# A gated cross-attention and feed-forward block: order of GpSimd's sums and statistics, of one copy on ScalarE and of two normalizations on VectorE

## What is computed

```python
x = x + jnp.tanh(g_xattn[0]) * xattn(layernorm(x), ctx, Wq, bq, Wk, bk)
x = x + jnp.tanh(g_ffn[0]) * ffn(layernorm(x), W_up, W_gate, W_down)

def xattn(logits, features, Wq, bq, Wk, bk):
    query = einsum('bnc,dc->bnd', features, Wq) + bq
    key = einsum('bnc,dc->bnd', features, Wk) + bk
    attention = softmax(einsum('bnd,bmd->bnm', query, key), axis=-1)
    return einsum('bln,bmn->blm', logits, attention)

def ffn(x, W_up, W_gate, W_down):   # each weight w rounded to sign * mean(|w|), or 0
    up, gate = einsum('bsd,ed->bse', x, wu), einsum('bsd,ed->bse', x, wg)
    return einsum('bse,de->bsd', silu(up) * gate, wd)
```

## Time and profile before

| | us |
|---|---|
| median of three runs | 396.83 (396.21 to 397.08) |
| profiled execution, its own time | 397.08 |
| its span | 395.3 |
| TensorE busy | 389.9 (99%) |
| VectorE busy | 314.4 (80%) |
| ScalarE busy | 266.7 (67%) |
| GpSimd busy | 169.3 (43%) |

### The profile page before, as it was taken

How to read it: one execution, slowest core, us unless ns; L and a number is a source line. 1 busy time by engine, 2 the same in 40 slices (tenths; PEclk the granted TensorE clock), 3 DMA queues, 4 the chain that set the end, 5 groups by cost and what they waited for, 6 DMA issues and landing times.

```text
span 395.3 us, 6059 instructions
## 1 busy us (share of the span) xinstructions
PE 389.9 (99%) x1944; PEld 214.9 (54%) x1952; DVE 314.4 (80%) x475; ACT 266.7 (67%) x360; POOL 169.3 (43%) x187
## 2 busy tenths in 40 slices
PE   8999999999999999999999999999999999999997
PEld 6566775454444444444444444444445565656886
DVE  0768897888899985879897875786869989798974
ACT  3786989889778786869788863746377566654400
POOL 0686826657875013222347002435359446271000
PEclk9999999999999999999999999999999999999999
DMA  7999967598500030030009643041500000000014
GB/s 286 409 413 414 389 210 174 151 266 211 162 2 0 1 108 0 2 107 0 2 0 225 117 79 61 1 167 73 165 22 1 2 2 2 0 2 0 2 55 159
DMA packets 43183, 43.91 MB, mean 111 GB/s; under 512 B 30992, under 2 KB 33168, under 8 KB 41104
## 3 DMA queue, kind: packets, MB, share of 16 engines
q1 hardware_dynamic: 43152, 43.53, 35.4%
HBM read 29.89 MB, written 6.29 MB: 92 GB/s over the span
## 4 chain that ended last, share of the span: by engine, by line
PE 75%; DVE 7%; issue 6%; ACT 5%; POOL 3%; DMA 2%; SPq 1%; DVEq 0%; POOLq 0%; ACTq 0%
PE pair L872 22%; PE pair L874 22%; PE pair L946 14%; PE pair L990 11%; PE pair L788 3%; DMA xf<-in_wdT 2%; PE pair L738 1%; ACT sh L1102 1%; DVE small L1473 1%; PE pair L724 1%; PE pair L803 1%; DMA xf<-in_first 1%; SPq L466 1%; DVE small L1515 1%; DVE xf L1674 1%
## 5 line engine op out<-in xcount | busy, mean ns | idle before, releaser
L872 PE MATMUL pair<-xb_hi,w_sb 128*128 128x512 f16 x448 | 169.8, 379 | 0.4 <-ACT xf L1299 0.2
L874 PE MATMUL pair<-xb_lo,w_sb 128*128 128x512 f16 x448 | 169.8, 379 | 0.0
L872 PEld LDWEIGHTS pair<-xb_hi,w_sb 128*128 128x128 bf16 x448 | 43.8, 98 | 52.9 <-ACT xf L1299 1.1
L874 PEld LDWEIGHTS pair<-xb_lo,w_sb 128*128 128x128 bf16 x448 | 43.8, 98 | 51.1 <-issue 0.3
L1250 ACT ACTIVATE xf<-xf,small 128x512 f32<-128x512 f32 x48 | 34.5, 720 | 52.3 <-DVE xf L1669 31.6
L946 PE MATMUL pair<-x_sb,sh 128*128 128x512 bf16 x248 | 55.1, 379 | 0.4
L1674 DVE SCALAR_TENSOR_TENSOR xf<-xf,small 128x512 f32<-128x512 f32 x48 | 40.0, 836 | 8.4 <-ACT xf L1250 8.4
L946 PEld LDWEIGHTS pair<-x_sb,sh 128*128 128x128 f16 x256 | 24.9, 98 | 30.6 <-DVE x_sb L1711 0.9
L604 POOL TENSOR_TENSOR w_sb<-w_sb 128x512 bf16<-128x512 bf16 x8 | 9.6, 1197 | 63.0 <-ACT w_sb L1124 63.0
L1679 DVE TENSOR_TENSOR sh<-xf,sh 128x512 f16<-128x512 f32 x36 | 32.1, 898 | 0.7 <-ACT sh L1261 0.7
L1725 DVE SCALAR_TENSOR_TENSOR x_sb<-pair,small,x_sb 128x256 f32<-128x256 f32 (+1 forms) x57 | 25.5, 472 | 5.9 <-PE pair L990 5.4
(11 more groups left out here) (198 smaller groups left out, 715.9 us busy)
## 6 DMA issues: line engine op xcount, KB each, us to landing
w_sb<-in_wugT SPq DMA_DIRECT2D x8, 1024.0 KB, 14.7
x_sb<-in_x SPq DMA_DIRECT2D x4, 1024.0 KB, 11.3
xf<-in_wdT SPq DMA_DIRECT2D x4, 1024.0 KB, 6.6
xt_sb<-in_wdT SPq DMA_DIRECT2D x4, 1024.0 KB, 5.0
xt_sb<-in_xT SPq DMA_DIRECT2D x12, 256.0 KB, 6.1
x_dram<-x_sb SPq DMA_DIRECT2D x8, 256.0 KB, 3.3
out<-x_sb SPq DMA_DIRECT2D x8, 256.0 KB, 2.0
x_sb<-x_dram SPq DMA_DIRECT2D x2, 1024.0 KB, 5.5
```

Source lines behind the costliest of these rows:

```text
L872: pe.matmul(dst[:, m * 512:(m + 1) * 512], w[:, o:o + P], hi[:, k], start=start and k == 0, stop=False, skip_group_check=not start)
L874: last = pe.matmul(dst[:, m * 512:(m + 1) * 512], w[:, o:o + P], lo[:, k], start=False, stop=k == 1, skip_group_check=not start)
```

## The change

It touches no computation, only the order of steps on three engines. On GpSimd the four sums of x are made in one go, in the order in which the products need them (XA follows), and the wait for `s_pn0` between them goes. In batch 1 the second pair of both layer norms, `rstd1_two(1, 1)` and `rstd2_two(0, 1)`, comes before the sums of p. The T1 difference goes from behind T3 to the second round of the loop of batch 2. On ScalarE the copy of T1 goes ahead of `exp_row(3, 2)`. On VectorE `norm_x1(0, 2)` and `norm_x1(0, 3)` go ahead of two reciprocals of batch 2.

```diff
--- before.py
+++ after.py
@@ -251,7 +251,7 @@
         MIX = (1, 5, 6, 3, 7, 2, 4)
         MIX_TO = {1: (0, 0), 5: (1, 1), 6: (0, 1), 3: (0, 1), 7: (1, 1), 2: (0, 0), 4: (1, 0)}
         MIX_BEFORE = {2: 1, 3: 6, 7: 5}
-        XA = {1: (0, 0), 2: (0, 1), 4: (1, 1), 5: 0, 7: 1, 6: 2, 3: 3}
+        XA = {1: (0, 0), 2: (0, 1), 4: (1, 1), 5: 0, 6: 1, 3: 2, 7: 3}
         PB = {1: (0, 0), 2: (1, 0), 3: (1, 1), 5: 0, 6: 1, 7: 2, 4: 3}
 
         def x_quarter(b, lh, nh):
@@ -568,17 +568,15 @@
                 step(pool.tensor_scalar(ve2[:, two], mv2[:, own, 1], LN_EPS, 1.0 / XS ** 2, ALU.add, ALU.mult))
                 pool.tensor_tensor(r2[:, own], ve2[:, two], mhalf, ALU.pow).then_inc(s_r2, 2)
 
-            def x_sums_1(b):
+            def x_sums(b):
                 for i in range(NT):
                     pool.wait_ge(*xt_in(b, i))
                 pool.tensor_tensor(x_sum(b, 0), x_quarter(b, 1, 0), x_quarter(b, 1, 1), ALU.add).then_inc(s_ss, 1)
-                pool.tensor_tensor(x_sum(b, 1), x_quarter(b, 0, 0), x_quarter(b, 1, 0), ALU.subtract).then_inc(s_ss, 1)
-
-            def x_sums_2(b):
                 hold(pool, s_ss, 4 * b + 1)
-                pool.tensor_tensor(x_sum(b, 2), x_sum(b, 0), x_quarter(b, 0, 0), ALU.subtract).then_inc(s_ss, 1)
-                hold(pool, s_ss, 4 * b + 3)
-                pool.tensor_tensor(x_sum(b, 3), x_quarter(b, 0, 1), x_sum(b, 2), ALU.subtract).then_inc(s_ss, 1)
+                pool.tensor_tensor(x_sum(b, 1), x_sum(b, 0), x_quarter(b, 0, 0), ALU.subtract).then_inc(s_ss, 1)
+                hold(pool, s_ss, 4 * b + 2)
+                pool.tensor_tensor(x_sum(b, 2), x_quarter(b, 0, 1), x_sum(b, 1), ALU.subtract).then_inc(s_ss, 1)
+                pool.tensor_tensor(x_sum(b, 3), x_quarter(b, 0, 0), x_quarter(b, 1, 0), ALU.subtract).then_inc(s_ss, 1)
 
             def p_sums_1(b):
                 hold(pool, s_at, b * NT + NT)
@@ -616,31 +614,29 @@
 
             pool.wait_ge(s_tanh, 1)
             pool.wait_ge(s_const, 4)
-            x_sums_1(0)
-            hold(pool, s_pn0, NT - 1)
-            x_sums_2(0)
+            x_sums(0)
             rstd1_two(0, 0)
             p_sums_1(0)
             rstd1_two(0, 1)
             p_sums_2(0)
-            x_sums_1(1)
-            x_sums_2(1)
+            x_sums(1)
             rstd1_two(1, 0)
             rstd2_two(0, 0)
+            rstd1_two(1, 1)
+            rstd2_two(0, 1)
             p_sums_1(1)
-            rstd1_two(1, 1)
             p_sums_2(1)
-            rstd2_two(0, 1)
             rstd1(2, 0)
             rstd1(2, 1)
             rstd2_two(1, 0)
             rstd2_two(1, 1)
             hold(pool, s_x2n, 2 * NT)
             pool.tensor_tensor(t3_sb, xf_half(1, 1), xf_half(1, 0), ALU.subtract).then_inc(s_t3, 1)
-            hold(pool, s_t3, 1)
-            pool.tensor_tensor(xf_half(1, 0), xf_half(1, 0), xf_half(0, 0), ALU.subtract).then_inc(s_t1, 1)
             for b in range(NS, NB - 1):
                 for i in range(NT):
+                    if i == 1:
+                        hold(pool, s_t3, 1)
+                        pool.tensor_tensor(xf_half(1, 0), xf_half(1, 0), xf_half(0, 0), ALU.subtract).then_inc(s_t1, 1)
                     rstd2(b, i)
                     if i + 2 < NT:
                         rstd1(b, i + 2)
@@ -1195,15 +1191,15 @@
                         if b == 1 and i == 2:
                             act.wait_ge(s_x2n, NT)
                             high_t(0, "B11", xf_half(0, 0))
+                        if b == 2 and i == 1:
+                            act.wait_ge(s_t1, 1)
+                            high_t(0, "T1", xf_half(1, 0))
                         exp_row(b + 1, i + 1)
                         if b == 2 and i == 2:
                             copy_at(b + 1, NT - 2)
                             norm_p(b + 1, NT - 1)
                         if i == 1:
                             norm_p(b + 1, 2)
-                        if b == 2 and i == 1:
-                            act.wait_ge(s_t1, 1)
-                            high_t(0, "T1", xf_half(1, 0))
 
                     if first and i in (0, NT - 1):
                         sum_abs(0, 2 + (i > 0))
@@ -1574,14 +1570,14 @@
                 add_mixed(b, 1)
                 row_max(b + 1, 0)
                 row_max(b + 1, 1)
+                if b == 1:
+                    norm_x1(0, 2)
+                    norm_x1(0, 3)
                 row_rsum(b + 1, 0)
                 row_rsum(b + 1, 1)
                 add_mixed(b, 5)
                 rows_in(b + 1, 0)
                 add_mixed(b, 6)
-                if b == 1:
-                    norm_x1(0, 2)
-                    norm_x1(0, 3)
                 row_max(b + 1, 2)
                 rows_in(b + 1, 1)
                 add_mixed(b, 3)
```

## The result

The changed kernel took a median of 400.35 us (399.96 to 401.18, four runs) beside 396.65 for the kernel before (four runs): a ratio of 1.0095, 95% interval 1.0083 to 1.0107. That is 3.70 us slower, by the interval 3.3 to 4.2. The profiled execution took 400.03 for a span of 398.2, with a granted clock of 1.0. The lines have new numbers: the product of the probabilities is L1555 (L1559 before), the first sum of p L583 (L585), T1 L639 (L641), the transposes L745 (L749), the products L784 (L788), exponential and scaling L1098 and L1103, the rounding to 16 bits L1139, the reciprocal L1473, the statistics L1486.

A forecast was written before the change was run, and what follows sets the result against it. The prediction took TensorE, busy 389.9 of 395.3 us, to set the end. Profiled 397.08 - 0.10 + 1.69 + 2.45 = 401.12, or 400.9 against the median of 396.83; range 399.0 to 401.8.

The forecast's parts named there:

- place 1: GpSimd's sums of x in batch 0 made in one go: 0.1 us gained, as they hold up VectorE's products.
- place 2: Second rstd pairs ahead of batch 1's sums of p on GpSimd: TensorE waits 1.60 us, plus 0.09 for restart.
- place 3: norm_x1(0, 2) and (0, 3) ahead of VectorE's reciprocals: costs nothing, covered by the hole of place 2; without it about 0.4.
- place 4: Later T1 on GpSimd, its copy ahead of ScalarE's exponential: TensorE 2.45 us late at the transposes near 79 us.
- The reading as shared bandwidth: Rival at place 1: no exclusive lock between VectorE and GpSimd, most of 0.95 us gained; total 400.0, no chance given.
- only place 4 costs: Rival: batch 1's fourth row tile statistic finished before 38.1, so place 2 costs nothing; 399.2 us, chance 0.04.
- nothing taken back: After 80 us the order is the old one and engines enter equally late, so none of the delay is recovered.
- The slip of SP's queue: Rival: late T3 and T1 meet SP's queue, delaying feed-forward entry by 1 to 2 us more; 402.4, chance 0.07.

The follow-up runs named there:

- experiment 5: The changed kernel with norm_x1(0, 2) and norm_x1(0, 3) back at their old place on VectorE: 400.20 us, ratio 1.0090 to the kernel before.
- experiment 6: The kernel before with the sums of x in one go and new order, batch 0's fourth held behind VectorE's third product: 396.40 us, ratio 0.9992.
- experiment 8: experiment 6 plus T1 behind rstd1(2, 2) on GpSimd, the coefficients one round later, ScalarE's order as before: 396.71 us, ratio 0.9997 to the kernel before.
- experiment 9: experiment 6 with VectorE's remainder of B21 moved behind two normalizations of batch 1: 396.32 us, ratio 1.0000 to the kernel before.
- experiment 7: The changed kernel with only rstd1_two(1, 1) back behind the first sums of p: 398.60 us, ratio 1.0049 to the kernel before.
- experiment 2: The kernel before with only both second rstd pairs put ahead of the sums of p in batch 1: 398.03 us, ratio 1.0027.
- experiment 4: The kernel before with only T1 moved behind the coefficients on GpSimd, ScalarE's order as before: 397.97 us, ratio 1.0032.
- experiment 1: The kernel before with only the sums of x made in one go and in the new order: 396.06 us, ratio 0.9984.
- experiment 3: The kernel before with only T1 later on GpSimd and its copy ahead of the exponential on ScalarE: 399.19 us, ratio 1.0055.
- experiment 10: experiment 1 with VectorE's remainder of B21 moved behind two normalizations of batch 1: 396.67 us, ratio 1.0008 to the kernel before.

## Why the prediction held, and where its terms were off

The forecast was 400.9, with 399.0 to 401.8; measured 400.35. Term by term, from the holes by starts, with 0.06 to 0.09 for each restart:

| term | predicted | changed kernel's trace | alone, by medians |
|---|---|---|---|
| place 1 | -0.10 | +0.06 | -0.64 (-1.0 to -0.2) |
| place 2 | +1.69 | +1.79 | +1.33 (0.7 to 1.5) |
| place 3 | 0 | 0 | 0 (experiment 5) |
| place 4 | +2.45 | +2.31 | +2.49 (1.6 to 2.8) |
| sum | +4.04 | +4.16 | +3.18 |

**Place 1** held in mechanism; that its size held in the trace is partly luck. The lock makes products one and three twice as long, the third 0.55 longer than alone, and TensorE loses before the transposes what it no longer loses before product 5. All four sums start where the prediction put them, less 0.4, by which x was loaded earlier in this execution; VectorE's products came 0.64 earlier with the shorter start. Another pair of shifts gives another size: in the five traces with the sums in one go the holes of batch 0, that at 25 us left out, are 0.70 to 1.65. The cause is shown by all twelve traces together: with a sum beside it the third product took 1.03 or 1.04 (five traces), without one 0.49 (seven, experiments 6, 8 and 9 among them, where the fourth sum was held back). The Trainium skill's rule that the prediction leaned on (SBUF — State Buffer, section on its two separate sides: the pair of ports is an exclusive lock for the whole instruction) is borne out for these products; of VectorE's instructions with one input the page says it only for certain fast modes, and no row tells in which mode these run. The reading as shared bandwidth, worth 0.95, would have had TensorE without a hole here. By medians place 1 is worth a little more than the trace shows, and the reason for that isn't settled.

**Place 2** held: from the statistic's end (39.10) to the sum's start (42.80) 3.70, worked out as 43.26 less 39.68 = 3.58, and TensorE's hole 1.71 for 1.60, with 0.08 for the restart. The rival "only place 4 costs" needed the statistic before 38.1; it came with no idle time before it, as read. Experiment 7 shows that the pair behind this wait is the whole cost. The medians of experiment 2 give less than the trace, 1.33 with 1.5 at most, and that stays open.

**Place 3** held, by experiment 5. The prediction's reason, that place 2's hole covers it, is not tested by this, since experiment 5 has that hole too.

**Place 4** held in both holes: 1.32 and 1.09, forecast as 1.3 and 1.1. One step of the working has a slip: a scaling that comes at 75.79 and takes 0.72 ends at 76.51, not 76.44, so the first wait comes to 1.4. It changes only the split, not the 2.45. The term is mis-sized by little. The prediction counted 2.45; the holes with their restarts are 2.53, and the 0.22 that TensorE lost in before at 79.20 (0.16 and 0.06) is part of them, so 2.31 were new. Experiment 4 splits it by medians, some 1.3 for GpSimd's order and, by subtraction, 1.2 for ScalarE's. The prediction had put all on the exponential and had not seen that T1 ahead of the next rstd2 costs TensorE by itself.

**The sum and "nothing taken back".** The changed kernel has 4.16 of new holes by places, the medians differ by 3.70 with 3.3 to 4.2 for the interval. The single places add up to 3.18 by medians, each with 0.2 to 0.9 to either side. The hole of 0.35 that the profiled execution of before had at 100.95, at the entry into the feed-forward stage, is in neither the changed kernel nor experiments 1 to 5. It went even where TensorE was delayed by nothing (experiment 1), so it was probably a chance of that execution, which was also 0.43 above the median. Else TensorE's order and holes behind 85 us are the same, as forecast. The slip of SP's queue, the rival of 402.4, did not happen.

## What to carry to other kernels

Ask of every step that waits what stands behind it on its own engine: a chain that waits for a late statistic, put ahead of a sum that TensorE needs, costs its wait (2.29 here) and the length of all steps ahead of the sum (3.53), less what GpSimd had to spare (4.1 of the 5.8 were covered, 1.7 were not). The shorter pair alone, with a wait of 1.43, stayed within that cover and cost nothing (experiment 7). When two engines are to be kept off each other's memory, look for the next neighbour before moving an instruction: the remainder of B21 left one collision for another, which put the chain behind it 0.6 later. And a single profile of a kernel with a varying start is read by its holes, since its total can lie 0.7 to 0.9 to either side of the median (experiments 3, 6 and 8). Even the holes of its first stage are to be compared over several traces, since they move with the start and with the loads.

## What the runs showed of the hardware

- **The lock works both ways and down to the smallest instruction.** A GpSimd step with two numbers per partition took 0.81 us in eight executions and 1.95 in two, beside the same VectorE instruction of 1.22 with two inputs from memory, and in the second case it ended 0.55 after that instruction, although it had begun 0.18 before it. A GpSimd difference of 128x1024 that began 0.22 to 0.23 after that instruction took 3.21 instead of 2.37 (experiments 9 and 10). With that VectorE instruction moved away (experiments 9 and 10) it took 0.81. I had counted only long GpSimd steps against VectorE. The Trainium skill has the condition in SBUF — State Buffer, section on its two separate sides, where a VectorE instruction with two SBUF inputs is among those that take the pair against a GpSimd one that reads SBUF. By the page the one that starts first keeps it; the 1.95 went to a step that had started first, and there the traces differ from the page.
- **A waiting instruction gets in between two that are back to back.** In the changed kernel the third sum ends at 14.39, VectorE's held product at 14.67, and the fourth sum, which waits for nothing, takes 1.46 instead of 1.27. A sum that followed another without a wait took 1.45 or 1.46 in all seven traces in which a product was being held at that moment, and 1.27 or 1.28 in the two in which none was (before, experiment 4). The third sum, which starts 0.15 after the second, took 1.27 in the changed kernel although the first product had just been held. So GpSimd pays 0.19 only where its sums lie back to back.
- **TensorE's start differs from execution to execution.** Its second group of matmuls, the same eight records, in before, the changed kernel and experiment 1:

```profile
4.01 3.27 PE L803 MATMUL pair<-xf 128*128 128x256 f32 x8
```

```profile
3.97 2.67 PE L799 MATMUL pair<-xf 128*128 128x256 f32 x8
```

```profile
3.88 2.00 PE L798 MATMUL pair<-xf 128*128 128x256 f32 x8
```

Those with 256 columns stand 0.43 apart at first and 0.22 later; the change came at 7.1, at about 5.4 and at 4.2 us. The granted clock is 1.00 in every stretch of the first 10 us, in before as in experiment 1, so the rows don't say what made it.
